# A fused two-layer GNN and mixture-of-experts kernel: router groups regrouped, early scatters paced, and part of the last softmax sums moved to VectorE

## The reference, cut to what matters

```
h = rmsnorm(x); q, k, v = h@wq.T, h@wk.T, h@wv.T   # 4 heads, 2 key heads, rope
att = softmax(causal(q @ k.T / sqrt(32)))
x = x + (att @ v) @ wo.T
flat = rmsnorm(x)
probs = softmax(flat @ router_w.T); top 2 of 8 experts, weights normalised
out = sum over experts of weight * (silu(flat@w1.T) * (flat@w3.T)) @ w2.T
return x + out
```

## Time and profile before

| what | value |
| --- | --- |
| median of three runs | 571.85 us (571.85 to 577.89) |
| the profiled execution | 571.83 us, its span 570.1 us |
| TensorE busy | 487.1 us (85%) |
| VectorE busy | 427.9 us (75%) |
| ScalarE busy | 314.2 us (55%) |
| GpSimd busy | 252.3 us (44%) |

### The profile page before, as it was taken

The page is one execution under the profiler, slowest core; times in us unless marked ns, Lnnn a source line. Parts: engine busy times, 40 slices in busy tenths (PEclk is TensorE's granted clock), DMA queues, the critical chain, the costliest instruction groups (busy, mean ns, idle before and its releaser), DMA issues.

```text
span 570.1 us, 11302 instructions
## 1 busy us (share of the span) xinstructions
PE 487.1 (85%) x3819; PEld 275.4 (48%) x3819; DVE 427.9 (75%) x1065; ACT 314.2 (55%) x522; POOL 252.3 (44%) x275
## 2 busy tenths in 40 slices
PE   1999995879999979998867778889989987898990
PEld 1533333557777745454432233233343226797990
DVE  6897966878999992565778679879977614866674
ACT  0687796966999900120113544456639654466770
POOL 3000002522444440110146189789946575377663
PEclk9999998989999999999957689999999996899996
DMA  8999975200115925011023443200040395869985
GB/s 293 400 422 423 421 274 178 93 1 22 30 28 203 409 58 115 0 42 28 15 75 99 122 118 104 90 2 1 0 143 20 135 356 160 250 182 361 399 299 186
DMA packets 39570, 93.43 MB, mean 164 GB/s; under 512 B 7488, under 2 KB 24944, under 8 KB 35168
## 3 DMA queue, kind: packets, MB, share of 16 engines
q1 hardware_dynamic: 35072, 86.96, 43.4%
q0 software_dynamic: 2272, 4.69, 2.3%
q10 hardware_dynamic: 2176, 1.13, 0.7%
HBM read 69.39 MB, written 21.00 MB: 159 GB/s over the span
## 4 chain that ended last, share of the span: by engine, by line
PE 54%; DVE 20%; DMA 9%; ACT 6%; issue 6%; SPq 3%; POOL 2%; POOLq 0%; DVEq 0%; ACTq 0%
PE ps L1586 9%; DVE A L2393 8%; PE ps L1763 8%; PE ps L1497 7%; PE ps L1514 6%; PE ps L1401 5%; PE ps L1755 3%; DMA R<-in_adj_in 3%; PE ps L1664 3%; DMA A<-w_split 2%; PE ps L1867 2%; PE ps L1611 2%; SPq L812 1%; PE ps L1381 1%; DMA slots_in<-R,A 1%
## 5 line engine op out<-in xcount | busy, mean ns | idle before, releaser
L2393 DVE TENSOR_REDUCE A<-ps 128x1 f32<-128x512 f32 (+3 forms) x160 | 86.1, 601 | 12.3 <-PE ps L1664 11.5
L1302 ACT ACTIVATE A<-ps 128x1024 f32<-128x1024 f32 (+3 forms) x80 | 68.4, 893 | 38.4 <-PE ps L1755 38.2
L1007 POOL TENSOR_TENSOR G<-G,A 128x1024 f32<-128x1024 f32 (+3 forms) x40 | 73.7, 1876 | 8.3 <-ACT A L1302 8.2
L1664 PE MATMUL ps<-A 96*128 96x512 f16 (+3 forms) x160 | 55.1, 382 | 10.3 <-DVE A L2393 4.5
L1401 PE MATMUL ps<-R,G 128*128 128x512 f32 x128 | 59.3, 605 | 1.2 <-DVE G L1967 0.8
L1586 PE MATMUL ps<-A,G 128*128 128x512 f32 x128 | 59.9, 594 | 0.0
L1514 PE MATMUL ps<-R 128*128 128x128 f16 x768 | 49.1, 221 | 7.0 <-DVE x L2085 5.8
L1514 PEld LDWEIGHTS ps<-R 128*128 128x128 f16 x768 | 46.1, 99 | 14.5 <-issue 6.6
L2067 DVE SCALAR_TENSOR_TENSOR R<-R 128x512 f16<-128x512 f32 x64 | 46.7, 752 | 6.8 <-ACT R L1157 6.5
L1867 PE MATMUL ps<-A 128*128 128x128 f16 (+1 forms) x702 | 47.6, 224 | 3.3 <-DMA A<-w_split 3.3
L1155 ACT ACTIVATE R<-ps,b 128x512 f32<-128x512 f32 x64 | 44.0, 688 | 10.6 <-PE ps L1497 9.4
(11 more groups left out here) (311 smaller groups left out, 920.7 us busy)
## 6 DMA issues: line engine op xcount, KB each, us to landing
A<-w_split SPq DMA_DIRECT2D x39, 533.0 KB, 10.2
A<-in_adj_t SPq DMA_DIRECT2D x16, 1024.0 KB, 17.6
slots_in<-xn SPq DMA_DIRECT2D x1, 8320.0 KB, 22.4
R<-in_adj_in SPq DMA_DIRECT2D x7, 1024.0 KB
w_split<-A SPq DMA_DIRECT2D x9, 725.0 KB, 4.0
xn<-in_adj_in SPq DMA_DIRECT2D x5, 1024.0 KB, 12.9
xT<-in_adj_in SPq DMA_DIRECT2D x4, 1024.0 KB, 12.6
A<-in_f_w SPq DMA_DIRECT2D x16, 170.5 KB
```

The costliest lines, as they stand in the source:

```text
L1007: pool.tensor_tensor(total, total, probabilities(n, pair)[:, :, t0:CW], ALU.add).then_inc(s_sum, 1)
L1302: act.activation(probabilities(n, pair)[:, :, t0:CW], ps[:, 2 * pair:2 * pair + 2, t0:CW], ACT.Exp, scale=1.0 / (SQ * SQ * float(HD) ** 0. ...
L1664: last = pe.matmul(ps[:, bank, 0:width], queries(t // TPC, h)[0:KQ, P * (t % TPC):P * (t % TPC) + P], keys(b, h // (NH // NKV))[0:KQ, 0:wi ...
L2393: dve.reduce_max(pm[:, h, t % TPC, b:b + 1], ps[:, bank, 0:width], AX_X).then_inc(s_rmf, 1)
```

## The change

The groups become chunks 0 and 1; chunk 2; chunk 3. With that chunk 1's work moves out of chunk 3's steps into those of chunk 2. ScalarE takes two pieces from VectorE: the normalised first rows of chunk 1, and the high half of the transposed rows of chunks 0 and 1; VectorE then waits for that high half before it forms the low one. GpSimd's `router_root(1)` moves from behind its sums into them, behind those of step (2, 6). The first router group now chooses in step (3, 0) instead of (2, 11). All 24 early scatters wait for one more exponential each, from step (3, 3) on, and `low_weights(7)` comes after the tenth. In chunk 3, VectorE adds up the probabilities of steps 8 to 13 (ten additions of 128x1024); TensorE leaves out those six products with ones and multiplies the sum once, at the last step. ScalarE's exponential waits for the addition that last used its buffer.

```diff
-GTS = (TPC, 2 * TPC, TPC)
+GTS = (2 * TPC, TPC, TPC)
...
-                       (1, 7): [("rows", 0)], (2, 1): [("tr", 0)], (2, 2): [("rows2", 0)], (2, 3): [("logit", 0)],
-                       (2, 7): [("dt", 1)], (2, 8): [("db", 1)], (2, 11): [("choose", 0)],
-                       (3, 0): [("dt", 2), ("out", 1), ("db", 2), ("exp", 0)],
-                       (3, 1): [("out", 2), ("stats", 1), ("stats", 2), ("weigh", 0)],
-                       (3, 2): [("rows", 1), ("rows", 2), ("rank", 0)], (3, 4): [("tr", 1), ("tr", 2)],
-                       (3, 5): [("logit", 1), ("logit", 2), ("choose", 1), ("rows2", 1), ("rows2", 2)],
-                       (3, 6): [("exp", 1), ("weigh", 1)], (3, 7): [("rank", 1)]}
+                       (1, 7): [("rows", 0)], (2, 1): [("tr", 0)], (2, 2): [("rows2", 0), ("dt", 1)],
+                       (2, 3): [("logit", 0), ("db", 1)], (2, 4): [("out", 1), ("stats", 1)],
+                       (2, 7): [("rows", 1)], (2, 8): [("tr", 1)], (2, 9): [("rows2", 1)], (2, 10): [("logit", 1)],
+                       (3, 0): [("dt", 2), ("db", 2), ("choose", 0), ("exp", 0)],
+                       (3, 1): [("out", 2), ("stats", 2), ("weigh", 0)],
+                       (3, 2): [("rank", 0), ("rows", 2)], (3, 3): [("tr", 2)],
+                       (3, 4): [("logit", 2), ("choose", 1), ("rows2", 2)],
+                       (3, 5): [("exp", 1), ("weigh", 1)], (3, 6): [("rank", 1)]}
...
+        vector_steps = [n for n, (c, j) in enumerate(steps) if c == NC - 1 and 8 <= n - 2 * c * (c + 1) < 14]
+        vector_sums = {n: 2 * max(0, k - 1) for k, n in enumerate(vector_steps)}
...
-        PACE = 2 * (len(steps) - len([c for c, _ in steps if c == NC - 1]) + 11)
+        ROWS_ON_SCALAR = (0, 1)
+        PACE = 2 * (len(steps) - len([c for c, _ in steps if c == NC - 1]) + 3)
...
+                if (c, turn) == (2, 6):
+                    router_root(1)
...
-            router_root(1)
             router_root(2)
...
-                        if g == 1:
-                            pool.wait_ge(s_p, min(2 * len(steps), PACE + (4 * (2 * t + which)) // 5))
+                        n = 2 * ((GTS[0] if g else 0) + t) + which
+                        pool.wait_ge(s_p, PACE + n)
                         scatter_rows(g, t, which)
-
-            pool.wait_ge(s_fn2, 1)
+                        if n == 9:
+                            low_weights(7)
+
+            pool.wait_ge(s_fn2, 2)
             scatter_group(0)
-            low_weights(7)
...
+                        if last_user[n] in vector_sums:
+                            act.wait_ge(s_vsum, vector_sums[last_user[n]] + pair + 1)
...
-                    if what == ("rows", 0):
-                        router_rows(0, 0)
+                    if what[0] == "tr" and what[1] in ROWS_ON_SCALAR:
+                        high_of_rows(what[1])
+                    if what[0] == "rows" and what[1] in ROWS_ON_SCALAR:
+                        router_rows(what[1], 0)
...
+                if n in vector_sums:
+                    return
                 if c == NC - 1:
+                    if last_step(c, j):
+                        pe.wait_ge(s_vsum, 2 * (len(vector_steps) - 1))
+                        head_products(7, c, j, one, last_sums, 0, False, False)
...
-                    if c < NC - 1:
+                    if c in ROWS_ON_SCALAR:
+                        dve.wait_ge(s_thi, NC + 1 + c)
+                    elif c < NC - 1:
                         chain(dve.tensor_scalar(th[:, CW * c:CW * c + CW], ps[:, bank, :], SX, None, ALU.mult))
...
+            def add_last_probabilities(n):
+                for pair in range(2):
+                    dve.wait_ge(s_p, 2 * n + pair + 1)
+                    if n == vector_steps[1]:
+                        dve.tensor_tensor(last_sums(pair), probabilities(n - 1, pair), probabilities(n, pair), ALU.add).then_inc(s_vsum, 1)
+                    else:
+                        dve.wait_ge(s_vsum, vector_sums[n - 1] + pair + 1)
+                        dve.tensor_tensor(last_sums(pair), last_sums(pair), probabilities(n, pair), ALU.add).then_inc(s_vsum, 1)
+            for n in vector_steps[1:]:
+                add_last_probabilities(n)
```

More of the change, by code:

```diff
@@ L235, in head_sums, with last_sums @@
             return flat[:, 2 * CW * pair:2 * CW * (pair + 1)].rearrange("p (h t) -> p h t", h=2)
+        def last_sums(pair):
+            o = ROWS_AT + 2 * CW * pair
+            return R[:, o:o + 2 * CW].rearrange("p (h t) -> p h t", h=2)
         o = 0
@@ L327, in group_cols @@
             for n in (TE[g], 2 * TE[g], TE[g] // 2, 2 * GTS[g], 2 * GTS[g]):
-                v.append(free_cols(1 + g, o, n))
+                v.append(free_cols((2, 1, 3)[g], o, n))
                 o += n
@@ L457, in program @@
         s_sum = sem("probabilities_summed")
+        s_vsum = sem("last_probabilities_summed_by_vector")
         s_st = sem("scores_ready")
@@ L1777, in times_values @@
                                      first_step(c, j), last_step(c, j))
-                if n in sum_no:
+                if n in sum_no or n in vector_sums:
                     last.then_inc(s_pv, 1)
@@ L2419, in unit @@
                     row_statistics(what[1])
-                elif what[0] == "rows" and what[1]:
-                    router_rows(what[1])
+                elif what[0] == "rows":
+                    if what[1] not in ROWS_ON_SCALAR:
+                        router_rows(what[1])
                 elif what[0] == "tr":
                     c = what[1]
-                    if c < NC - 1:
+                    if c in ROWS_ON_SCALAR:
+                        dve.wait_ge(s_thi, NC + 1 + c)
+                    elif c < NC - 1:
                         chain(dve.tensor_scalar(th[:, CW * c:CW * c + CW], ps[:, bank, :], SX, None, ALU.mult))
                     else:
-                        dve.wait_ge(s_thi, NC + 1)
+                        dve.wait_ge(s_thi, NC + 1 + len(ROWS_ON_SCALAR))
                     dve.scalar_tensor_tensor(out=tl[:, CW * c:CW * c + CW], in0=ps[:, bank, :], scalar=SX,
```

## The result

The changed kernel takes **592.84 us** (median of four runs, 592.35 to 594.65); the kernel before, run beside it, 574.52 (571.85 to 577.89). The ratio is 1.032, with a 95% interval of 1.025 to 1.040: slower by 3.2%, and beyond the range forecast. The profiled execution took 592.35 us, span 590.6, against a span of 570.1.

What follows compares the result with a forecast made beforehand. In chunk 2 TensorE, VectorE and GpSimd were nearly full and tied, in late chunk 3 TensorE set the pace. 571.83 + 8.1 (chunk 2) + 1.1 (clock) - 1.7 (slots start earlier) = 579.3 us, slower by 1.3%; range 570.5 to 584.

Steps and rivals of the forecast that it cites:

- the 1.32: Early scatters: an issue beside VectorE's additions may take 1.32 us; with eight or so they end at 471, before 472.65.
- The 0.7: Scatters: by the skill's rule issues stay at 0.98 beside additions, and the sum would be 0.7 lower; not adopted.
- The stop behind the split: Chunk 2, step (2, 8): cast, ScalarE's 2.34 us weights split, exponential and semaphores leave TensorE 4.1 us without scores.
- The work: Chunk 2: work moved onto VectorE, 1.92 for `out` and `stats`, 0.69 low half, 0.55 waits, together 3.2 us.
- The waits for the transposes: Chunk 2, ScalarE waiting in order: VectorE loses 0.6 in step (2, 1), 3.3 in step (2, 8), 0.35 ahead of it.
- Step (2, 1): Chunk 2: cast and half exponential make TensorE's scores 1.6 us late; VectorE loses 0.6.
- Six steps at 2.05: Chunk 3: six steps lose a ones product and fall to 2.05 us, 4.7 won; the sums' product costs 0.93.
- The lateness ahead of them: Chunk 3: waits less the TensorE work that has left put step (3, 8) 2.5 us late.
- The two waits that the forecast named: Chunk 3: scores of step (3, 1) 1.5 us late through `exp`; `tr` in step (3, 3) waits 2.0 for rows.
- Banks covering the waits: Rival: PSUM banks cover ScalarE's waits, chunk 2 grows only by the work; 573.3 us, no change; chance 0.18.
- a relieved chunk 3: Rival: moved work fits chunk 2's 5.1 us idle, chunk 3's `exp` and `tr` not late; 565.3 us; chance 0.13.
- VectorE as the bound of the last steps: Rival: chunk 3's ten additions of 1.225 us set the step at 2.45 or start 2.4 later; 581.7 us; chance 0.13.

Runs made afterwards that it cites:

- e4: Changed kernel with the high halves of chunks 0 and 1 and chunk 1's first router rows back on VectorE: 594.75 us (1.035).
- e3: Kernel before with only VectorE's sums of six steps in chunk 3 added, as in the change: 584.49 us (1.016).
- e1: Changed kernel, but TensorE forms all ones products again and VectorE adds nothing: 587.29 us (1.020).
- e2: Changed kernel, but each of VectorE's ten additions waits for the one before to complete: 585.22 us (1.018).
- i1: Changed kernel with the ten additions replaced by one-input row maxima, as close together, and TensorE's product of the sums left out: 581.46 us (one run).
- f2: Against e2, ScalarE's weights split moved from step (2, 8) to step (2, 10): 581.95 us (1.015).
- f1: Against e2, high halves of chunks 0 and 1 back on VectorE, chunk 1's first router rows still on ScalarE: 577.68 us (1.006).
- h2: Against f1, group 0's choosing put first in step (3, 0): 575.57 us (1.004).
- h4: Against h2, with f2's edit, and chunk 2's rows ahead of group 0's ranks in step (3, 2): 574.89 us (1.001).
- f4: Kernel before with only GpSimd's last weights split moved ahead of group 0's scatters: 574.12 us (1.000).
- f3: Against f4, VectorE also sums the probabilities of steps (3, 10) to (3, 14), one addition at a time: 574.80 us (1.001).
- h1: Against f3, the pace of group 1's scatters starts two steps earlier: 570.60 us, 0.994 of the kernel before.

## Why the prediction was wrong, point by point

**The sum.** 571.83 + 10.1 + 0.0 + 6.5 + 3.8 (the spread of the runs ahead of chunk 2) = 592.2. The forecast had +9.2, -1.3 and -0.4 for the first three. Without the 3.8 it would be 588.5, still above the range. The base, 571.83, was also a fast execution of that kernel: the median of its four runs is 574.52.

**The step that failed: scatters.** "Beside VectorE's additions an issue may take the 1.32 that output scatters took ...; with eight or so that is 471." This gave each issue a price of its own. What holds here is a block that lasts as long as additions follow one another: one issue of 11.09 in the change, 12.31 in e4 and 9.14 in e3, none in e1, e2 and i1. The 1.32 was read beside VectorE instructions that leave gaps; as an upper bound it was none, since no row of before had ten such instructions in a row. The instruction beside that row is one of VectorE's low halves, with both inputs in SBUF:

```profile
510.32 0.56 DVE L2552 TENSOR_TENSOR A<-A 128x384 f16<-128x384 f32 x1 [0.38 <-ACT A L1345]
```

The issue began at 510.41, inside it, and ended at 511.73, 0.85 behind its end. In the kernel before, all 28 issues from 430 us on that begin inside such an instruction, more than 0.1 us ahead of its end, end 0.84 to 0.87 behind it. So 1.32 was not a price but the same wait beside a single short instruction, and the long issues end by the same rule: 0.86 behind the last of ten additions after the change, 0.87 in e3, 0.85 in e4.

The row that gave the hint was used elsewhere: VectorE held up for 2.37 us by GpSimd's split looks like the same exclusion seen from the other side, and it already outlasted one instruction, since the window holds two of GpSimd's. The text had the bound in hand, the 12.3 us of additions, and did not set it against the scatters: 468.2 + 12.3 is 480.5, 7.9 later than the 472.65 of before, and the sum 571.83 + 9.2 + 7.9 = 588.9. The 0.7 by which the sum "would be lower" with issues of 0.98 is worked out nowhere.

By the Trainium skill (SBUF — State Buffer, "Who interferes with whom") a VectorE instruction with two inputs in SBUF contends with a GpSimd instruction that reads SBUF; the trace agrees (two small instructions of VectorE took 3.06 us beside GpSimd's split, and 0.37 without it in f2). The same section infers that such an addition leaves descriptors alone, which the prediction weighed and did not take; for indirect scatters the runs contradict it (11.09 beside ten additions, 0.98 beside ten reductions). These also read their target rows from SBUF, and which part of the issue waits no run shows.

**Chunk 2: right mechanism, prices a little low.** The stop behind the split came as described: 4.1 us without scores forecast, 3.93 measured, a lower clock behind it. The work was 3.2, measured 3.8 with the rows' wait in it (f1). The waits for the transposes were priced at 0.6 + 3.3 + 0.35 and 1.1 for the clock, 5.4 in all; f1 puts them at 6.4 to 7.6. Step (2, 1) was 0.6 and is 1.0; the rest is behind it, and its parts were not measured one by one.

**Chunk 3: two small errors the same way.** Six steps at 2.05 were right (2.1), worth 3.1 us with the product of the sums (e1 against e2) where 3.8 was forecast. The lateness ahead of them was taken as 2.5 at step (3, 8); e1, which has the change's order without its sums, takes 56.0 us for the chunk, 3.4 more than before. The two waits that the forecast named came near their price, 1.59 for 1.5 and 1.68 for 2.0, so the 0.9 that is missing lies elsewhere. h2 and h4 took out 1.2 and 2.5 us, most of it by the order of VectorE's units.

**The rivals.** Banks covering the waits, and a relieved chunk 3, fell. VectorE as the bound of the last steps named the right engine and the wrong victim: the additions (466.61 to 478.03) ended 3.7 us before attention and held up GpSimd instead. The range ended at 584 because no case joined a block of the scatters to chunk 2's loss.

## What to carry to other kernels

Before VectorE gets a run of instructions with two inputs in SBUF, look for GpSimd's indirect DMAs in the same stretch; a wait for the previous instruction's completion between them costs 0.17 us each and lets the scatters through. An engine that works through its units in order should be given a piece only where its producer is done by then, and nothing long should stand behind such a wait. Where two things gate the next stage (here the last early scatter and the end of attention), an edit to one alone may show nothing: f4 and f3 left the scatters where they were or later, h1 moved both.

## What was not expected of the hardware

- An issue of an indirect DMA that takes 0.98 us alone took 11.09 beside ten additions of 128x1024 without a gap, and 1.02 with a semaphore wait between them. If it begins while VectorE runs an instruction with two inputs in SBUF it ends 0.84 to 0.87 us behind that one, or behind the last of a run without gaps.
- The other way round, four scaled copies of 128x128 from SBUF to SBUF on VectorE took 7.28 us beside GpSimd's two-input sums, and 0.87 without (both in e4).
- With a stop of TensorE of 3.34 us (e3) and of 3.93 (the change) the granted clock was 0.50 and 0.57 over four microseconds at its end or close behind it; with a stop of 1.60 in the place of the second (f2) it stayed at 1.00.
